# Second mixing stage: the reciprocals of the denominators as a power with exponent -1 on GpSimd

## The reference, cut to what matters

```python
def _aft_local(emb, wq, bq, wk, bk, wv, bv, wo, bo, pos_bias):
    q, k, v = emb @ wq + bq, emb @ wk + bk, emb @ wv + bv
    mask = |i - j| < 128
    w = pos_bias * mask
    ek = exp(k - max_over_positions(k)); ew = exp(w - max_over_columns(w))
    num = einsum('tj,bjd->btd', ew, ek * v)
    den = einsum('tj,bjd->btd', ew, ek)
    y = sigmoid(q) * num / den
    return y @ wo + bo
```

## Time and profile before

| | us |
|---|---|
| median of 3 runs | 3303.51 (3299.11 to 3306.58) |
| the profiled execution's own time | 3309.8 |
| its span | 3308.2 |
| PE busy in the span | 3063.4 |
| DVE busy in the span | 2330.2 |
| ACT busy in the span | 1806.8 |
| POOL busy in the span | 1073.4 |

### The profile page before, as it was taken

How to read it: one execution, slowest core, us unless ns; L and a number is a source line. 1 busy time by engine, 2 the same in 40 slices (tenths; PEclk the granted TensorE clock), 3 DMA queues, 4 the chain that set the end, 5 groups by cost and what they waited for, 6 DMA issues and landing times. The chain is left out here.

```text
span 3308.2 us, 57696 instructions
## 1 busy us (share of the span) xinstructions
PE 3063.4 (93%) x19234; PEld 2297.5 (69%) x19234; DVE 2330.2 (70%) x4173; ACT 1806.8 (55%) x3126; POOL 1073.4 (32%) x949
## 2 busy tenths in 40 slices
PE   6999799999999999999996899899999999768887
PEld 5777577777777777678875777688888888634443
DVE  5563688888888888665553798944555544589996
ACT  3332699999999999622323232232222222159995
POOL 3343332232232223154542355520111110016666
PEclk9999899999999999999997999999999999889999
DMA  6775322232232222365644444421111111301112
GB/s 207 242 249 183 109 86 65 64 95 67 63 94 69 62 79 84 121 223 199 230 179 151 148 141 136 144 89 45 45 45 42 44 44 33 112 4 58 64 46 77
DMA packets 239797, 350.52 MB, mean 106 GB/s; under 512 B 32240, under 2 KB 129552, under 8 KB 239632
## 3 DMA queue, kind: packets, MB, share of 16 engines
q1 hardware_dynamic: 208704, 290.41, 27.3%
q0 software_dynamic: 8912, 32.82, 3.0%
q10 hardware_dynamic: 22016, 25.17, 2.1%
HBM read 210.68 MB, written 137.64 MB: 105 GB/s over the span
## 5 line engine op out<-in xcount | busy, mean ns | idle before, releaser
L913 DVE CUSTOM_DVE_ANT_0 attend_probs<-attend_scores,attend_bias_table 128x1024 f32<-128x1024 f32 x512 | 622.8, 1217 | 111.3 <-PE attend_scores L754 100.5
L833 ACT ACTIVATE attend_probs<-attend_probs,attend_neg_max 128x1024 f32<-128x1024 f32 x512 | 592.7, 1158 | 89.0 <-DVE attend_neg_max L913 85.4
L770 PE MATMUL attend_turned<-ident,attend_probs 128*128 128x128 f32 x4096 | 549.8, 274 | 1.7 <-ACT attend_probsT L842 1.5
L770 PEld LDWEIGHTS attend_turned<-ident,attend_probs 128*128 128x128 f32 x4096 | 477.3, 140 | 90.5 <-ACT attend_probsT L842 14.5
L754 PE MATMUL attend_scores<-attend_k_stack,attend_q_stack 96*128 96x512 f32 x1024 | 367.8, 441 | 15.8 <-DMA attend_q_stack<-qk_parts 15.8
L842 ACT COPY attend_probsT<-attend_turned 128x512 f32<-128x512 f32 x640 | 357.9, 579 | 1.1 <-PE attend_turned L770 1.0
L2319 DVE TENSOR_TENSOR cross_ffn_h_lo<-cross_ffn_hidden,cross_ffn_h_hi 128x512 fp32r<-128x512 f32 x128 | 104.4, 821 | 337.6 <-ACT cross_ffn_h_hi L2210 337.0
L716 POOL TENSOR_TENSOR attend_out_parts<-attend_out_full,attend_out_parts 128x256 fp32r<-128x256 f32 x64 | 46.7, 730 | 755.6 <-ACT attend_out_parts L850 755.6
L785 PE MATMUL attend_out_acc<-attend_probsT,attend_v_in 128*32 128x256 f32 x4096 | 273.7, 385 | 0.7 <-DVE attend_out_full L933 0.7
L922 DVE COPY attend_probsT<-attend_turned 128x512 f32<-128x512 f32 x384 | 262.7, 684 | 2.3 <-PE attend_turned L770 2.1
L2207 ACT ACTIVATE cross_ffn_hidden<-cross_ffn_h_acc,cross_ffn_b_cols 128x512 f32<-128x512 f32 x128 | 88.3, 690 | 268.8 <-PE cross_ffn_h_acc L2114 246.0
(11 more groups left out here) (304 smaller groups left out, 6677.7 us busy)
## 6 DMA issues: line engine op xcount, KB each, us to landing
qk_parts<-qkv_qk_out SPq DMA_DIRECT2D x64, 512.0 KB, 3.2
attend_k_stack<-qk_parts SPq DMA_DIRECT2D x192, 128.0 KB, 2.5
attend_q_stack<-qk_parts SPq DMA_DIRECT2D x192, 128.0 KB, 2.7
qkv_wq_raw<-L_ffn_w POOLq DMA_DIRECT2D x16, 1024.0 KB, 7.8
o_parts<-attend_out_parts ACTq DMA_DIRECT2D x64, 256.0 KB, 2.5
carried_o_in<-o_parts SPq DMA_DIRECT2D x48, 256.0 KB, 4.6
qkv_x_in<-x SPq DMA_DIRECT2D x8, 1024.0 KB, 5.7
v_rows<-qkv_v_out SPq DMA_DIRECT2D x32, 256.0 KB, 3.4
```

The source lines that it names most:

```text
L770: last = pe.transpose(turned[:, bank, c], probs[:, i % 4, k * P:(k + 1) * P], ident[:, :])
L833: act.activation(probs[:, i % 4], probs[:, i % 4], ACT.Exp, bias=neg_max[:, i % 4:i % 4 + 1], scale=-1.0, accum_out=den[:, qg % 2, j, h:h ...
L913: dve.tensor_tensor_reduce(probs[:, i % 4], scores[:, i % 2], bias_table[:, h, at:at + T], -1.0, BIG, ALU.add, ALU.min, neg_max[:, i % 4:i ...
```

## The change

POOL gets a tile of one column that holds -1, and a function `invert`, which raises `recip` to the power -1 in place. It stands in POOL's body after the two `split_e` of a step and ahead of `scale_and_shift` and `widen_sums`. It waits for `read["den"]`, the semaphore that DVE's multiply into `recip` (L1842) counts up, and counts up `recip_step`, for which DVE already waits ahead of the multiply into `y`. DVE's reciprocal and the wait ahead of it go.

```diff
+        minus_one = sb("minus_one", [P, 1])
...
             pool.memset(zero[:, :], 0.0).then_inc(setup_step, 1)
+            pool.memset(minus_one[:, :], -1.0).then_inc(setup_step, 1)
             pool.memset(sums_wide[:, :, :, :, :], 0.0).then_inc(setup_step, 1)
-            pool.wait_ge(setup_step, 2)
+            pool.wait_ge(setup_step, 3)
...
+            def invert(b, t):
+                i = b * TB + t
+                pool.wait_ge(read["den"], i + 1)
+                pool.tensor_tensor(recip[:, :], recip[:, :], minus_one[:, :].to_broadcast([P, D]), ALU.pow).then_inc(recip_step, 1)
...
                         split_e(*ahead, 0)
                         split_e(*ahead, 1)
 
+                    invert(b, s)
                     if s in (0, 1) and not first:
                         scale_and_shift(b - 1, 0, range(2 * s, 2 * s + 2))
...
                 dve.scalar_tensor_tensor(out=recip[:, :], in0=expq_in[:, t % 4], scalar=1.0, in1=acc[:, bank_of("den", t)],
                                          op0=ALU.add, op1=ALU.mult).then_inc(read["den"], 1)
-                dve.wait_ge(read["den"], i + 1)
-                dve.reciprocal(recip[:, :], recip[:, :]).then_inc(recip_step, 1)
                 dve.wait_ge(recip_step, i + 1)
                 dve.wait_ge(ready["num"], i + 1)
                 dve.tensor_tensor(y[:, t % 4], acc[:, bank_of("num", t)], recip[:, :], ALU.mult).then_inc(read["num"], 1)
```

## The result

| | us |
|---|---|
| median before | 3303.03 |
| median after | 5896.85 (5896.09 to 5900.35, 4 runs) |
| ratio | 1.7851, 95% interval 1.783 to 1.7872 |
| forecast, with its range | 3600 (3365 to 4100) |
| span of the profiled execution before and after | 3308.2, 5895.2 |

The sign was right and the size was far off: the time grew by 2594 us, nine times what was forecast, and lies outside the range.

What follows compares the result with a forecast made beforehand. PE and DVE were taken to bound the stage in turns, and the loop through POOL's power to bound it afterwards. 32 powers of 10 us less 26.5 gave +293 us, hence 3600 us (3365 to 4100).

Steps and rivals of the forecast that it cites:

- What bounds the kernel before: Stage around `recip`: PE and DVE take turns; removing DVE's 3.35 us a step at no price wins 20 to 30 us.
- The loop through the power: From power to power through DVE's residual add, PE, ACT and POOL's subtract: a plain step takes the power plus 7.2 us.
- Its sum beside the powers: Time of the stage's 31 gaps without the powers: 232.5 us at full clock, 263.1 us with slow starts.
- The sum with d: Change of the stage, d being one power's duration: 32 d - 26.5 us with slow starts, 32 d - 57 at full clock.
- TensorE's clock: PE restarts at 1.2 GHz after each pause: +1.6 us for the denominator, +0.2 for transposes, plain steps 9.0 us beside the power.
- The price of a power: One power on POOL over `recip`: taken as 10 us, with 1.3 and 27 us kept as ends.
- the scale of ratios: Estimates for POOL's power: 6.4 us from DVE's reciprocal-to-multiply ratio, 18 us from 14 small Newton instructions at 1.30 us.
- the upper end: POOL's power as two polynomials of about ten multiply-adds each, every one a whole pass: 21 x 1.30 = 27 us.
- The rival of a very slow power: POOL's powers over 26 us, partly worked one value at a time: at 27 us +838, 4141 us, open above; chance 0.09.

Runs made afterwards that it cites:

- the eight multiplies: Changed kernel with eight multiplies by a column of 1, each waiting for the last, in place of the power on GpSimd; no reciprocal taken: 3560.1 us, ratio 1.0783.
- moving one link: Changed kernel with VectorE's residual of an older tile (add, statistics, inverse root) moved ahead of its wait for the power: 5814.7 us.
- d = 1.04: Changed kernel with one multiply by a column of 1 in place of the power on GpSimd, no reciprocal taken: 3290.8 us against 3301.6, ratio 0.9964.

## Why the prediction was wrong

**What bounds the kernel before: right.** DVE and PE took turns, and what DVE's 3.35 us a step were worth was put at 20 to 30 us; with them taken away by ScalarE it is 31, and 27.6 in the stage's gaps (286.2 to 258.6).

**The loop through the power: right from 9 us a power upwards.** Its links are in the timeline after, and it was tested with powers of 41.1 and 81.9 us, with the eight multiplies, and by moving one link. Its sum beside the powers was 263.1 us; 255.7, 258.1 and, with the eight multiplies, 533.3 - 31 x 8.87 = 258.3 were measured. The sum with d = 81.93, 32 x 81.93 - 26.5 = +2595 us, against +2594 between the medians. Part of that agreement is luck: between the two profiled executions the span grew by 2587, so the gaps were 7 us too long in the sum, and the execution before that was profiled happened to lie 7 us above its median. Single gaps were off both ways. Those that go through PE took 7.8 to 9.7 us where the sum has 9.0 to 10.3: plain ones 9.3 for 9.0, the ones ahead of a sequence's last tile 7.8 for 9.0, because its denominator has six matmuls of L1734 and not nine. At d = 1.04 the sum promised 13 us more than was won.

**TensorE's clock: right, and sized a little low.** In the timelines, from the first matmul of the denominator to the transposes took 2.0 us more after a pause (4.43 us, both with the power and with the eight multiplies, against 2.39), where the prediction had added 1.6; and without the clock term the eight multiplies would come out 31 us too low.

**The price of a power: wrong, and alone the cause.** The step says "I take d = 10 us, between 6.4 and 18 on the scale of ratios, and keep 1.3 and 27". It is 81.93 us, three times the upper end. The forecast error, 5897 - 3600, is 32 x (81.93 - 10) = 2302 us to within 5. The upper end was made of 21 passes at the price of a subtract. A whole subtract costs 1.30 us for 512 columns, 0.0025 us a column, and the power costs 0.159 us a column, 63 such passes; what fills them, no run here shows. Nothing in the trace before could bound it from above, and I let three numbers built from neighbouring rows look like bounds. The rival of a very slow power had a chance of 0.09, and was priced at 27 us "and open above", without a number there. Its size came true, its reason in part not: a power over one partition takes as long as over 128, so the values of a column are not worked out one after the other.

**The ratio between the engines.** For the power against VectorE's reciprocal the measured ratio is 81.93 / 3.353 = 24; for simple operations with two full tiles it is 1.9 to 2.0 (multiply 1.29 us on GpSimd and 0.69 on VectorE, add 1.38 and 0.68). The Trainium skill, GPSIMD Engine Reference, Elementwise — side-by-side cycle accounting, has GpSimd at half VectorE's speed for an add; the rows for simple operations agree, and the power does not follow it. The same section of the Trainium skill says that longer bodies are bound by their own operations, at roughly three a cycle; by that rate and its 1.2 GHz, 0.159 us a column would be an estimate of over 500 operations. The measurement goes that way, but no run here can show how many there are, or that they are the bound.

## What to carry to other kernels

An operation that no row shows has no upper bound: measure it alone, at two widths, before building a schedule around it; one run gave price per column, fixed price and what it does not depend on. Moving work to an idle engine is a question of what stands in the loop, not of load: a short operation on GpSimd in the same place gained 11 us (with the reciprocal left out), and the sum "n times d plus the links" came within 3 us of the medians from 8.9 to 82 us a power, once d was known. Below that another bound takes over, and the sum promises too much. When the busy engine's dear operation is to go, look at what each other engine does it with: here two passes on ScalarE took 1.28 us where VectorE's reciprocal takes 3.35, and TensorE became the bound.

## What the runs showed of the hardware

- A power of float32 on GpSimd takes 0.159 us a column and 0.3 to 0.4 us besides, the same for the exponents -1, +1, 2 and 0.5 and for 1, 8, 64 and 128 partitions: 81.93 us for 512 columns.
- A multiply on GpSimd with a broadcast column as its second operand, or with the same tile twice, took 1.04 us for 128x512; operations with two different full tiles took 1.29 to 1.38 on average in the kernel before.
- VectorE's reciprocal costs by the column too: 1.753 us for 256, 3.353 for 512.
- On ScalarE, one over the root of the absolute value took 0.645 us and a square 0.632 us for 128x512.
